# Half of the aggregation's depth by Strassen's scheme in a five-step graph network

## The reference

```python
for _ in range(5):
    s_in  = state @ in_W.T + in_b
    s_out = state @ out_W.T + out_b
    a_in, a_out = A @ s_in, A.T @ s_out
    a = concat([a_in, a_out, state])
    r = sigmoid(a @ r_W.T + r_b)
    z = sigmoid(a @ z_W.T + z_b)
    h = tanh(concat([a_in, a_out, r * state]) @ h_W.T + h_b)
    state = (1 - z) * state + z * h
out = layernorm(x + tanh(state @ o1_W.T + o1_b) @ o2_W.T + o2_b)
```

## Time and profile before

| | |
|---|---|
| runs | 678.75, 679.21, 679.65 us; median 679.21 |
| profiled execution, its own time | 678.97 us |
| its span | 676.8 us |
| mean granted TensorE clock | 0.995 |
| TensorE (matmuls) busy | 664.5 us, 98% |
| VectorE busy | 485.6 us, 72% |
| ScalarE busy | 240.3 us, 35% |
| GpSimd busy | 41.5 us, 6% |

### The profile page before, as it was taken

One profiled execution on the slowest core, in us unless ns is written; L12 is line 12 of the kernel. 1 busy time (PEld: TensorE's weight loads), 2 busy tenths in 40 slices (PEclk: granted clock), 3 DMA queues, 4 the chain that ended last, 5 costly groups with the idle time before them and its releaser, 6 DMA issues.

```text
span 676.8 us, 8324 instructions
## 1 busy us (share of the span) xinstructions
PE 664.5 (98%) x3004; PEld 552.5 (82%) x3004; DVE 485.6 (72%) x810; ACT 240.3 (35%) x370; POOL 41.5 (6%) x36
## 2 busy tenths in 40 slices
PE   8999999999999999999999999999999999999994
PEld 7888888878888888888888888888888888888883
DVE  4985867787577769946777896575788757564786
ACT  2973644541232225213141441222153122223645
POOL 0032022000101010000101000000000000000002
PEclk9999999999999999999999999999999999999998
DMA  8991631322300032200002321000134200000003
GB/s 293 371 315 48 208 124 54 60 63 34 123 17 15 31 47 64 35 12 0 31 0 58 66 35 27 0 31 0 41 60 86 32 1 1 0 1 1 0 1 127
DMA packets 91185, 42.50 MB, mean 63 GB/s; under 512 B 72081, under 2 KB 80913, under 8 KB 91153
## 3 DMA queue, kind: packets, MB, share of 16 engines
q1 hardware_dynamic: 91152, 42.10, 22.4%
HBM read 31.07 MB, written 8.39 MB: 58 GB/s over the span
## 4 chain that ended last, share of the span: by engine, by line
PE 93%; DVE 4%; ACT 1%; issue 1%; DMA 0%; DVEq 0%
PE bank L467 43%; PE bank L453 16%; PE bank L454 16%; PE bank L455 16%; PE bank L568 2%; PE bank L599 1%; DVE work L964 1%; PE bank L555 1%; DVE stats L1202 1%; DVE a L1195 0%; DMA a<-in_L_gnn_r_W_dram 0%; DVE ring L884 0%; ACT work L705 0%; ACT a L868 0%; DVE work L970 0%
## 5 line engine op out<-in xcount | busy, mean ns | idle before, releaser
L467 PE MATMUL bank<-ring,rows 128*128 128x512 f32 x1280 | 292.7, 389 | 0.0
L467 PEld LDWEIGHTS bank<-ring,rows 128*128 128x128 f32 x1280 | 240.2, 188 | 49.9
L705 ACT ACTIVATE work<-work,bias 128x512 f32<-128x512 f32 x120 | 86.8, 724 | 285.5 <-DVE work L964 284.7
L964 DVE SCALAR_TENSOR_TENSOR work<-degree,deg_w,bank 128x512 f32<-128x512 uint16 x120 | 89.2, 744 | 117.9 <-PE bank L455 117.6
L453 PE MATMUL bank<-u_c,fold 128*128 128x512 f32 x240 | 93.9, 391 | 0.2 <-DVE work L964 0.2
L454 PE MATMUL bank<-u_c,fold 128*128 128x512 f32 x240 | 93.4, 389 | 0.0
L455 PE MATMUL bank<-u_c,fold 128*128 128x512 f32 x240 | 93.4, 389 | 0.0
L890 DVE CAST ring<-a 128x1024 fp32r<-128x1024 uint8 x128 | 88.2, 692 | 2.3 <-PE bank L467 2.3
L453 PE MATMUL bank<-st_c,own 128*128 128x512 f32 x160 | 62.3, 390 | 0.0
L455 PE MATMUL bank<-st_c,own 128*128 128x512 f32 x160 | 62.3, 389 | 0.0
L454 PE MATMUL bank<-st_c,own 128*128 128x512 f32 x160 | 62.2, 389 | 0.0
(11 more groups left out here) (121 smaller groups left out, 693.7 us busy)
## 6 DMA issues: line engine op xcount, KB each, us to landing
stage<-in_adj_dram SPq DMA_DIRECT2D x15, 512.0 KB, 7.1
res<-in_adj_dram SPq DMA_DIRECT2D x13, 512.0 KB, 6.0
turned_dram<-work SPq DMA_DIRECT2D x12, 512.0 KB, 2.6
rows<-turned_dram SPq DMA_DIRECT2D x192, 32.0 KB, 1.9
work<-in_x_dram SPq DMA_DIRECT2D x4, 512.0 KB, 9.6
rows<-work SPq DMA_DIRECT2D x64, 32.0 KB, 2.0
a<-in_adj_dram SPq DMA_DIRECT2D x3, 512.0 KB, 10.1
res<-in_x_dram SPq DMA_DIRECT2D x3, 512.0 KB, 4.5
```

The source lines that it names most:

```text
L467: last = nc.tensor.matmul(u_bank[2 * (c % 2) + d][:, :], rows[:, part, j, d * P:(d + 1) * P], ring[:, slot, jj, :], start=(j == 0 and part ...
L705: nc.scalar.activation(gates[:, g, e, :], gates[:, g, e, :], ACT.Tanh if g == H else ACT.Sigmoid, bias=bias[:, g, e:e + 1]).then_inc(gate_ ...
L964: nc.vector.scalar_tensor_tensor(out=gates[:, g, e, :], in0=degree[:, c * CW:(c + 1) * CW], scalar=deg_w[:, g, e:e + 1], in1=g_bank[s % 3] ...
```

## The change

In steps 1 to 4 the chunks are aggregated in pairs: side 0 is chunks 0 and 1, side 1 chunks 2 and 3. Of the depth, the half that is the rows of chunks 0 and 1 goes by Strassen's scheme (Winograd's form): seven products P1 to P7 of half-width blocks (128 state rows, 512 deep, 512 wide) take the place of eight. The other half, the rows of chunks 2 and 3, stays as it was. A pair has 22 entries (`ORDER`): fourteen of four matmuls and eight of eight. The stages of a step are now: chunks 0 and 1, gates of 0, gates of 1, chunks 2 and 3, gates of 2, gates of 3.

- The products need sums of adjacency blocks: three are formed once by GpSimd as bytes with an offset (`sum_blocks`) and cast with a bias that takes the offset off; the fourth is the two blocks added by VectorE while it casts (P5).
- They need sums of rows: four subtractions `t_add` on VectorE a step, split as the rows are. `ROWS_FIRST` and `ROWS_LATER` set where those operations stand between VectorE's gate sums, `HIGH_FIRST` and `HIGH_LATER` on ScalarE.
- The products are combined by one copy of P1 on ScalarE (`copy_p1`) and six additions on VectorE (`mix`).
- Of the 22 casts of a pair ScalarE now does twelve (P1, P2, P3, P4, P6, P7) and VectorE ten. ScalarE's first four for the next pair stand in the gates of the even chunk, after slot 3.
- SyncE keeps 12 of the 16 moves of chunk 3's rows, ScalarE issues 4. The rows of chunks 0 and 1 are loaded once P3 has been used.
- The output weights are stored to memory and loaded back at the end, and the residual's x is loaded after the last aggregation.

The core of the diff:

```diff
+    ORDER = [(P1, 0), (P6, 0), (P1, 1), (P6, 1), (P2, 0), (P2, 1), (P4, 0), (P4, 1), (P7, 0), (P7, 1), (P5, 0), (P5, 1),
+             (1, 4), (P3, 0), (0, 4), (P3, 1), (0, 5), (1, 5), (0, 6), (0, 7), (1, 6), (1, 7)]
+    BY_ACT = [n for n, (kind, _) in enumerate(ORDER) if kind in (P1, P2, P3, P4, P6, P7)]
+    ROWS = [(T1, 0), (T2, 0), ("b11", 0), (1, 0), (1, 1), (T4, 0), (T3, 0), (2, 0), (2, 1), (3, 0), (3, 1)]
...
 # SyncE: turn_move
-                for n in range(NQ):
+                for n in range(NQ - 1):
...
 # GpSimd: sum_blocks
+                for n, (out_, u, v, op) in enumerate(((a, a21, a22, ALU.add), (b, a, one, ALU.add), (s2, b, a11, ALU.subtract),
+                                                      (b, a11, one, ALU.add), (s3, b, a21, ALU.subtract),
+                                                      (b, a11, a12, ALU.add), (b, b, two, ALU.add), (s4, b, a, ALU.subtract))):
...
 # TensorE: aggregate_pair
+            def aggregate_pair(t, side):
+                pe.wait_ge(u_lo, t * S_TWO + side * 2 * TWO)
+                for n, (kind, p) in enumerate(ORDER):
+                    tile = ring[:, n % RING]
+                    if n in BY_ACT:
+                        pe.wait_ge(pair_ready, groups(t, side, len(BY_ACT), S_PAIR + BY_ACT.index(n) + 1))
+                    else:
+                        pe.wait_ge(std_cast, groups(t, side, len(BY_VECTOR), BY_VECTOR.index(n) + 1))
+                    if kind in BANK:
...
+                        if (kind, p) == (P2, 0):
+                            pe.wait_ge(p1_copied, groups(t, side, 1, 1))
+                        if (kind, p) == (P4, 0):
+                            pe.wait_ge(mixed, groups(t, side, 6, V))
+                        if (kind, p) == (P3, 0):
+                            pe.wait_ge(mixed, groups(t, side, 6, W5))
+                        for jj in range(2):
+                            for part in (HI, LO):
+                                last = nc.tensor.matmul(u_bank[BANK[kind]][:, :], product_rows(kind, part, 2 * p + jj), tile[:, jj, :],
...
 # ScalarE: cast, gate_chunk, aggregate_pair
+                if kind in (P6, P7, P3):
+                    nc.scalar.activation(ring[:, n % RING].rearrange("p j w -> p (j w)"), sums[:, side, m, h * 2 * CW:(h + 1) * 2 * CW],
+                                         ACT.Identity, bias=minus[:, m // 2:m // 2 + 1]).then_inc(pair_ready, 1)
+                else:
+                    high(ring[:, n % RING], a8[:, c, b + 2 * h:b + 2 * h + 2, :], pair_ready)
...
-                    if c == NC - 2 and s == 2 * DB - 1:
+                    if s == 2 * DB - 1 and (c == NC - 2 or c == 0 and not first):
                         for e in range(DB):
-                            split_state(t, NC - 1, e)
+                            split_state(t, c + 1, e)
                         for d in range(DB):
-                            split_u(t, NC - 1, d, first)
+                            split_u(t, c + 1, d, first)
+                        if c == 0:
+                            for k in range(RING):
+                                cast(t, 1, k)
+                        elif not last:
+                            for k in range(RING):
+                                cast(t + 1, 0, k)
...
+            def aggregate_pair(t, side):
+                cast(t, side, 4)
+                copy_p1(t, side)
+                for k in range(5, 8):
+                    cast(t, side, k)
+                if side == 0:
+                    for h in range(2):
+                        row_high(t, 2, h)
+                for k in range(8, 10):
+                    cast(t, side, k)
+                if side == 0:
+                    turn_move(t - 1)
+                for k in range(10, 12):
+                    cast(t, side, k)
+                for e in range(DB):
+                    split_state(t, 2 * side, e)
+                if side == 0:
+                    for h in range(2):
+                        row_high(t, 3, h)
+                for d in range(DB):
+                    split_u(t, 2 * side, d, False)
...
 # VectorE: gate_chunk, where the row operations stand
+            ROWS_LATER = {(2, 2): [("add", T1)], (2, 3): [("add", T2)], (3, 0): [("low", ROWS[0]), ("add", T4)],
+                          (3, 1): [("low", ROWS[1]), ("add", T3)], (3, 2): [("low", op) for op in ROWS[2:4]],
+                          (3, 3): [("low", ROWS[4])], (3, 4): [("low", ROWS[5])], (3, 5): [("low", ROWS[6])]}
...
+                elif c % 2 == 0:
+                    mix(t, c // 2, C21)
+                    mix(t, c // 2, C22)
-                if c == NC - 1:
+                if c == NC - 1 or c == 1 and not first:
                     update(t, c - 1)
                     if not last:
                         turn_state(t, c - 1)
                 gate(t, c, 0)
                 rs(t, c, 0)
-                rows_low(0, 0)
+                next_rows(0)
                 gate(t, c, 1)
                 rs_low(t, c, 0)
                 rs(t, c, 1)
-                rows_low(0, 1)
+                next_rows(1)
                 gate(t, c, 2)
```

More of the change, by code:

```diff
@@ L180, in fast_path @@
         turned_dram = nc.dram_tensor("turned_dram", [BY_DMA, NQ, SQ, NQ, BC * DB, SQ], F32, kind="Internal").ap()
+        o_dram = nc.dram_tensor("o_dram", [P, 4 * DB * D], F32, kind="Internal").ap()
+        partial = [stage[:, 2, n, :].bitcast(U32) for n in range(2)]
         u_bank = bank[0:4]
@@ L380, in _ @@
                 turn_store(t, 1)
+                for k in range(2):
+                    turn_load(t, k)
                 if t == LAST - 1:
@@ L460, in degrees, with multiply @@
                 nc.tensor.matmul(t_bank[:, :], ones_r[:, :], deg_part[:, :], start=True, stop=True).then_inc(degree_done, 1)
[L462 removed]
+            def multiply(c, p, d, tile, first, last, goes_on=False):
                 for jj in range(2):
                     j = 2 * p + jj
[L465 to L472 removed]
@@ new lines, in multiply, with aggregate @@
+                return m
+            def aggregate(t, c):
+                wait(pe, u_lo, (c - 1) * TWO)
+                pe.wait_ge(x_read, min(NC * DB, (c + 1) * TWO))
+                for p in range(NP):
+                    pe.wait_ge(pair_ready, c * NP + p + 1)
+                    if c == 0:
+                        pe.wait_ge(x_split, p // 2 + 1)
+                    for d in range(DB):
+                        last = multiply(c, p, d, ring[:, p % RING], p == 0, p == NP - 1)
+                        if p == NP - 1 and d == 0:
+                            last.then_inc(agg_done, 1)
+                    last.then_inc(pair_used, 1)
@@ L719, in gate_chunk @@
                 for s in range(GATE):
-                    if c == NC - 1 and s in (2, 3) and not last:
-                        row_high(t, 1, s - 2)
+                    if c == NC - 1 and not last:
+                        for op in (HIGH_FIRST if first else HIGH_LATER)[s]:
+                            row_high(t + 1, *op)
                     gate(t, c, s)
@@ L1023, in final, with next_rows @@
                         split_hidden(0)
+                def next_rows(n):
+                    if last or (c, n) not in (ROWS_FIRST if first else ROWS_LATER):
+                        return
+                    for what, k in (ROWS_FIRST if first else ROWS_LATER)[c, n]:
+                        if what == "add":
+                            t_add(t + 1, k)
+                        else:
+                            row_low(t + 1, *k)
                 if first:
@@ L1063, in gate_chunk @@
                 gate(t, c, 4)
+                next_rows(4)
                 if last and c == NC - 1:
```

472 lines of the change are left out of this document (319 added, 153 removed).

## The result

The changed kernel takes 700.62 us (median of 4 runs, 697.66 to 703.32), the kernel before 679.14 in the same comparison: a ratio of 1.0315, 95% interval 1.0273 to 1.0357. It is slower, as forecast, but by 21.5 us where 11.2 were forecast, and outside the range of 672 to 698.

A forecast was written before the change was run, and what follows sets the result against it. TensorE was taken to bound the kernel, busy 664.5 of 676.8 us. Terms: -14.5 + 8.0 + 3.7 + 10.8 + 3.2 = +11.2 on 678.97, with the median's 0.24 giving 690.4 us; range 672 to 698, main case 684 to 697.

The forecast's parts named there:

- Matmuls, -14.5: Aggregations of steps 1 to 4: 64 matmuls fewer at 0.2267 us each, 14.5 us gained if nothing waits.
- Start of an aggregation, +8.0: TensorE waits for ScalarE's late P7 casts: 1.5 us a step in side 0, 0.5 in side 1, 8.0 lost.
- Crossing to chunk 1, +3.7: Four early casts delay chunk 0's tanh pair and chunk 1's gate sums: 1.1 us in steps 1 to 3, 0.4 in step 4.
- Chunk 3, +10.8: Late gate sums make TensorE wait in chunk 3 of steps 1 to 3: 3.6 us each, 10.8 lost.
- both of its causes: In chunk 3: early casts ahead of chunk 2's tanh pair, and extra row operations before the second and third gate sums.
- Step 0, forecast +1.7 and +1.5: Step 0's chunk 3: 1.7 us by the late tanh pair, 1.5 by row operations delaying P1's split and the first mix.
- the sentence on GpSimd's byte sums under "at nothing": Step 0: byte sums end near 130.2 us, before the first cast needing them is due at 132.6, so cost nothing.
- Late residual loads, at nothing: At the end: late residual loads cost nothing, having a chunk stage of 72 matmuls, 16.3 us, above them.
- forecast -1.2: Step 4 with the tail, whole: 1.2 us shorter than in the kernel before.
- The clock, given 0.03 and 22 us: Rival: gaps halve TensorE's clock for 12 matmuls at each of eight crossings, 22 us more, 712 us; chance 0.03.
- "The clock held through all gaps of before": Argument against the falling-clock rival: the kernel before kept its clock through all its gaps.

The follow-up runs named there:

- tanh first: Changed kernel with ScalarE's four early casts of the next pair moved behind the even chunk's two tanh: 695.17 us, ratio 1.0233.
- GpSimd's work out: Changed kernel with GpSimd's byte sums replaced by tiny operations and most of its residual additions left out (output wrong): 691.98 us, ratio 1.0185.
- the second run of the changed kernel: The changed kernel measured once more, unchanged, to see where the clock falls: 700.14 us.
- rows behind P7: Changed kernel with chunk 2's row casts behind the P7 casts and its first row subtraction behind the P5 sums: 698.21 us, ratio 1.0275.
- rows later: Changed kernel with one row operation, not two, before each of chunk 3's second and third gate sums, ScalarE's row casts later: 695.50 us, ratio 1.0242.
- three orders: Changed kernel with early casts behind the tanh pair, one row operation before chunk 3's second and third gate sums, chunk 2's row casts behind P7's: 686.12 us.
- all orders: three orders plus side 0's early casts behind chunk 3's fourth and fifth gates, chunk 2's transposes, P1's copy and step 0's rows reordered: 689.49 us.
- casts split: all orders, but side 0's four early casts split: two behind chunk 2's tanh pair, one each behind chunk 3's third and fourth gate: 680.56 us.
- the last version: casts split with side 1's byte sums later, first four residual additions behind the last step's chunk 2 splits, other four once loaded: 672.05 us, ratio 0.9901.

## Why the prediction was wrong

The direction was right, and the terms that it summed for steps 1 to 3 held. **Matmuls, -14.5:** right; TensorE's entries keep their pitch, and a side of 120 x 0.2267 = 27.2 us was reached to 0.5. **Start of an aggregation, +8.0:** 1.6 and 0.5 measured for 1.5 and 0.5, and the order of row casts and P7 casts as its cause is shown (side 0 to 27.74). **Crossing to chunk 1, +3.7:** 1.1 in steps 1 to 3 and 0.5 in step 4, and shown. **Chunk 3, +10.8:** 3.8 where the clock held, for 3.6; both of its causes are shown, but not that the one goes without the other: with the tanh first, the sigmoid is late instead.

What failed:

**Step 0, forecast +1.7 and +1.5.** The stage took 6.8 more, and side 0 of step 1 is 0.4 longer than the others: 7.2 for 3.2. The step that failed is the sentence on GpSimd's byte sums under "at nothing": it asked only when they would be done, not what else they hold up. The question that it asked it answered rightly: the first cast of such a sum runs at 131.99 without a wait. Without GpSimd's work the stage is 4.0 shorter. The 2.8 over before that stay, with the wait for P1's split among them, and the 0.4 make 3.2, as forecast for the two terms together.

The trace of the kernel before held a sign of it (timeline, step 2; GpSimd's residual addition and VectorE's cast of 0.69):

```profile
283.27 1.67 POOL L433 TENSOR_TENSOR res<-res,o_bb 128x512 f32<-128x512 f32 x1 [42.59 <-DVE ring L890]
283.71 1.78 DVE L890 CAST ring<-a 128x1024 fp32r<-128x1024 uint8 x1
```

**Late residual loads, at nothing,** the same omission: the additions behind them cost the last step about 3 (forecast -1.2, measured +1.74; without them it is 3.1 shorter), and this cost moved with them through four kernels.

**The clock, given 0.03 and 22 us.** It fell, but not at eight crossings: in two of three steps, at 1.6 each, so 3.1, and once in step 0 behind the wait of 4.86, which is part of the 4.0 above. "The clock held through all gaps of before" was no evidence for gaps of 2.3 us, when before had none over 0.63 in the steps. The Trainium skill (TensorE: Matmul & The Clock Gate, HAM oscillation) says that waits of TensorE can bring its clock down to half. These traces agree, with 0.50 behind the 4.86 and two of the three waits of 2.31, but the 22 us that the prediction reckoned for it did not come.

The sum: 11.2 forecast, 22.2 measured between the two profiled spans; counted from each step's first matmul to the next, 5.0 more than forecast in step 0 (with the 1.5 counted to step 1), 0.8, 0.3 and 1.9 in steps 1 to 3, 3.0 in step 4 with the tail.

**Left open:** what decides whether the clock falls behind a wait of 2.31 us. Of steps 1 to 3 it fell in the first and third (the changed kernel, and GpSimd's work out), in the first (the second run of the changed kernel), in all three (tanh first), and in none (rows behind P7, with the same three waits). Behind the wait of 2.30 to 2.33 in the last step's crossing it fell in five kernels (tanh first, rows later, rows behind P7, three orders, all orders) and not in two (the changed kernel, both times, and casts split). No experiment here separates these. The spread of the times goes with it: the changed kernel's runs range over 5.7 us, the shortest at a mean granted clock of 0.993 and the longest at 0.986; those of the last version, with no such wait, range over 0.6. That the clock makes this spread is likely, not shown.

## What to carry to other kernels

An operation costed at nothing on an idle engine needs two questions: when it must be done, and which other engine's operations it stretches while it runs; look for the second in the trace wherever two engines overlap. Where an engine at half load serves several chains in order, list the chains that pass a new block of work at each place it could stand: here four casts of 4 us delayed a chain in three places and, split over three gaps, nothing in chunk 3 in the fourth. Try cures together before judging one: the first alone gained 5 us, all of them, with GpSimd's work moved, 28.

## What was unexpected in the hardware

Beside GpSimd's additions VectorE's operations on two operands of on-chip memory take mostly 1.5 to 1.8 us each, for 0.68 without them (some that meet an addition only in part take 0.7 to 1.3), its byte casts up to 1.78 for 0.69, its P5 pair 4.5 for 2.3; operations with one operand in a bank keep 0.64 to 0.75. No transpose of the state ran beside GpSimd. The Trainium skill says why such a pair may not overlap (SBUF — State Buffer, SBUF: two separate sides): VectorE, for operations with two inputs there or in a fast copy mode, and GpSimd share one pair of ports, which one instruction holds to its end. The numbers agree as far as they go: beside the last state update each operation lost 1.0 to 1.1 us, less than the 1.60 of one addition (6.39 / 4). No run shows in which mode the casts ran.

The second is the granted clock: 0.50 behind a wait of 2.31 us in some steps and 1.00 in others, with the same waits.
